# A second gather stage with ten slots, whose gather DMA adds onto loaded edge features

## The reference

```python
    def _L1_gnn_ref(x, edge_index, edge_attr, W, b, eps):
        src = edge_index[0]
        dst = edge_index[1]
        msg = jax.nn.relu(x[src] + edge_attr)
        agg = jax.ops.segment_sum(msg, dst, num_segments=x.shape[0])
        h = (1.0 + eps) * x + agg
        out = h @ W.T + b
        return jax.nn.relu(out)
...
    x = _layernorm(x + _L0_gnn_ref(x, edge_attr_64, ..., edge_index, batch0), axis=-1)
    x = _layernorm(x + _L1_gnn_ref(x, edge_index, edge_attr_64, L1_gnn_W, L1_gnn_b, L1_gnn_eps), axis=-1)
```

## Time and profile before

| | |
|---|---|
| time, median of 3 runs | 10885.92 us (10885.71 to 10889.72) |
| span of the profiled execution | 10892.7 us |
| second gather stage, first to last gather DMA | 6110.0 to 10760.8 us |
| GpSimd busy | 6799.3 us, 62% of the span |
| TensorE busy | 4140.9 us, 38% |
| VectorE busy | 2557.8 us, 23% |
| ScalarE busy | 1173.7 us, 11% |
| DMA engines, mean rate | 59 GB/s |

### The profile page before, as it was taken

How to read it: one execution, slowest core, us unless ns; L and a number is a source line. 1 busy time by engine, 2 the same in 40 slices (tenths; PEclk the granted TensorE clock), 3 DMA queues, 4 the chain that set the end, 5 groups by cost and what they waited for, 6 DMA issues and landing times. The chain is left out here.

```text
span 10892.7 us, 119855 instructions
## 1 busy us (share of the span) xinstructions
PE 4140.9 (38%) x36713; PEld 3322.5 (31%) x36713; DVE 2557.8 (23%) x7060; ACT 1173.7 (11%) x2055; POOL 6799.3 (62%) x6897
## 2 busy tenths in 40 slices
PE   4445444444444445445887311111111111111113
PEld 3333333333333333334776211111111111111112
DVE  2111111111111111114997311111111111111112
ACT  0000000000000000001334300000000000000001
POOL 5555555555555555556998466666666666666663
PEclk7655555656665655555555555555555555555555
DMA  2222222222222222222443111111111111111111
GB/s 78 60 61 61 61 61 60 61 61 61 61 61 61 61 60 61 61 61 75 125 123 114 50 44 44 43 45 44 44 44 44 44 43 45 44 43 45 44 44 35
DMA packets 882270, 637.83 MB, mean 59 GB/s; under 512 B 534579, under 2 KB 780831, under 8 KB 881496
## 3 DMA queue, kind: packets, MB, share of 16 engines
q1 hardware_dynamic: 590300, 326.49, 10.9%
q0 software_dynamic: 200416, 208.55, 10.2%
q10 hardware_dynamic: 91536, 102.58, 2.7%
HBM read 528.19 MB, written 108.90 MB: 58 GB/s over the span
## 5 line engine op out<-in xcount | busy, mean ns | idle before, releaser
L349 POOL DMA_INDIRECT Z<-in_x_dram,idx_ring x3125 | 2958.8, 947 | 2088.3 <-DVE idx_ring L526 1205.2
L1156 POOL DMA_INDIRECT X<-x_scratch,idx_ring x3125 | 2986.5, 956 | 1738.3 <-issue 893.5
L1185 PE MATMUL PS<-hot_c,msg_c 128*64 128x48 f32 x6250 | 811.6, 310 | 3865.8 <-ACT msg_c L1171 2630.0
L1185 PEld LDWEIGHTS PS<-hot_c,msg_c 128*64 128x64 f32 x6250 | 713.5, 223 | 3964.0 <-issue 2528.7
L401 PE MATMUL PS<-ZT,W_sb 128*64 128x256 f32 x2500 | 689.5, 647 | 2375.0 <-ACT ZT L451 2238.9
L515 DVE BATCH_NORM_STATS2 stats<-PS 128x320 f32 (+1 forms) x625 | 311.6, 499 | 3158.2 <-remote 2670.5
L1216 DVE TENSOR_TENSOR table<-table,PS 64x48 f32 x625 | 130.0, 208 | 3773.0 <-remote 1822.2
L401 PEld LDWEIGHTS PS<-ZT,W_sb 128*64 128x64 f32 x2500 | 183.7, 199 | 2637.2 <-ACT ZT L451 2488.9
L451 ACT ACTIVATE ZT<-PS 128x640 f32<-128x640 f32 x625 | 439.4, 703 | 4602.4 <-remote 4300.2
L391 PE MATMUL PS<-ident,Z 128*128 128x128 f32 x3125 | 845.7, 413 | 161.7 <-issue 158.6
L420 PE MATMUL PS<-W_sb,ZT 128*64 128x64 f32 x12500 | 877.7, 318 | 0.0
(11 more groups left out here) (140 smaller groups left out, 2682.9 us busy)
## 6 DMA issues: line engine op xcount, KB each, us to landing
Z<-in_edge_attr_dram SPq DMA_DIRECT2D x625, 160.0 KB
h_scratch<-h_ring ACTq DMA_DIRECT2D x625, 160.0 KB
h_turns<-h_scratch SPq DMA_DIRECT2D x125, 800.0 KB
E<-in_edge_attr_dram SPq DMA_DIRECT2D x625, 160.0 KB
Z<-in_x_dram,idx_ring POOLq DMA_INDIRECT x3125
X<-x_scratch,idx_ring POOLq DMA_INDIRECT x3125
x_nodes<-in_x_dram SPq DMA_DIRECT2D x1, 3125.0 KB
x_ring<-in_x_dram SPq DMA_DIRECT2D x25, 125.0 KB
```

Of the source, the lines that this page charges most:

```text
L349: nc.gpsimd.indirect_dma_start(out=Z[:, s, j, 0:D], out_offset=None, in_=x, in_offset=bass.IndirectOffsetOnAxis(ap=idx_ring[:, s, j:j + 1] ...
L1156: nc.gpsimd.indirect_dma_start(out=X[:, s, j, :], out_offset=None, in_=x1_dram, in_offset=bass.IndirectOffsetOnAxis(ap=idx_ring[:, s, j:j ...
L1185: last = nc.tensor.matmul(PS[D:P, s % 2, 0:WIN], msg[:, s, j, :], hot[:, s, j, :], start=(j == 0), stop=(j == TG - 1))
```

## The change

Only the second gather stage changes. The buffers E, msg and hot and the semaphores for loads and gathers have ten slots (RING) in place of five; X is gone. SyncE loads edge features up to ten groups ahead. GpSimd waits only until the edge features of its group have been loaded, and its indirect DMA, now with `compute_op=ALU.add`, adds the rows of x1 onto them in E. Its indices are read from `src_idx` where they lie, so its 3125 DMAs are written out one by one, without a loop, and `idx_ring` isn't used. ACT waits for the gather itself. DVE's add (L1208) and its index copy (L1211) are gone; DVE adds PE's result of a group onto the table five groups later, behind the one-hot matrix of the group now at hand. PE uses five PSUM banks. The other engines' loops cover two turns each (`loop_halves`).

```diff
-        gathered_x1 = [ctx.enter_context(nc.semaphore(f"gathered_x1{s}")) for s in range(S)]
+        gathered_x1 = [ctx.enter_context(nc.semaphore(f"gathered_x1{s}")) for s in range(2 * S)]
...
-            E = sb(here, "E", [P, S, TG, D])
-            X = sb(here, "X", [P, S, TG, D])
-            msg = sb(here, "msg_c", [P, S, TG, D])
-            hot = sb(here, "hot_c", [P, S, TG, WIN])
+            RING = 2 * S
+            E = sb(here, "E", [P, RING, TG, D])
+            msg = sb(here, "msg_c", [P, RING, TG, D])
+            hot = sb(here, "hot_c", [P, RING, TG, WIN])
...
                 @block.sync
-                        for s in range(S):
-                            reuse(sp, msg_ready[s], i)
-                            sp.dma_start(E[:, s, :, :], edge_v[i * S + s]).then_inc(e_loaded[s], 16)
+                        for s in range(S):
+                            r = half * S + s
+                            if later(i):
+                                sp.wait_ge(msg_ready, i * S + (s + 1 - RING))
+                            sp.dma_start(E[:, r, :, :], edge_v[i * S + s]).then_inc(e_loaded[r], 16)
...
                 @block.gpsimd
-                            reuse(pool, idx_ready[s], i)
-                            reuse(pool, sum_ready[s], i)
-                            carry_wait(pool)
-                            for j in range(TG):
-                                nc.gpsimd.indirect_dma_start(
-                                    out=X[:, s, j, :], out_offset=None, in_=x1_dram,
-                                    in_offset=bass.IndirectOffsetOnAxis(ap=idx_ring[:, s, j:j + 1], axis=0)
-                                ).then_inc(gathered[s], 16)
+                    for g in range(G):
+                        r = g % RING
+                        pool.wait_ge(e_loaded[r], 16 * (g // RING) + 16)
+                        carry_wait(pool)
+                        for j in range(TG):
+                            n = g * TG + j
+                            nc.gpsimd.indirect_dma_start(
+                                out=E[:, r, j, :], out_offset=None, in_=x1_dram,
+                                in_offset=bass.IndirectOffsetOnAxis(ap=src_idx[:, n:n + 1], axis=0),
+                                compute_op=ALU.add
+                            ).then_inc(gathered[r], 16)
...
                 @block.scalar
-                            act.wait_ge(sum_ready[s], i + 1)
-                            reuse(act, summed[s], i)
-                            act.activation(msg[:, s, :, :], E[:, s, :, :], ACT.Relu).then_inc(msg_ready[s], 1)
+                            act.wait_ge(gathered[r], n * (16 * TG) + 16 * TG)
+                            if later(i):
+                                act.wait_ge(summed, i * S + (s + 1 - RING))
+                            act.activation(msg[:, r, :, :], E[:, r, :, :], ACT.Relu).then_inc(msg_ready, 1)
...
                 @block.tensor
-                            reuse(pe, added, i * S + max(s - 1, 0))
+                            if not isinstance(i, int) or i >= 1:
+                                pe.wait_ge(added, i * S + (s + 1 - S))
                             for j in range(TG):
-                                last = nc.tensor.matmul(PS[D:P, s % 2, 0:WIN], msg[:, s, j, :], hot[:, s, j, :],
+                                last = nc.tensor.matmul(PS[D:P, s, 0:WIN], msg[:, r, j, :], hot[:, r, j, :],
                                                         start=(j == 0), stop=(j == TG - 1))
...
                 @block.vector
-                            dve.wait_ge(e_loaded[s], i * 16 + 16)
-                            dve.wait_ge(gathered[s], i * (16 * TG) + 16 * TG)
-                            nc.vector.tensor_tensor(E[:, s, :, :], X[:, s, :, :], E[:, s, :, :],
-                                                    ALU.add).then_inc(sum_ready[s], 1)
-
-                            nc.vector.tensor_copy(idx_ring[:, s, :],
-                                                  src_idx[:, ds(i * (S * TG) + (S + s) * TG, TG)]
-                                                  ).then_inc(idx_ready[s], 1)
+                    def turn(i, half, n):
                         firsts = windows_of_turn(dve)
                         for s in range(S):
+                            if s == S - 1:
+                                load_windows(dve, i)
+                            one_hot(i, half, s)
+                            add(i - 1, s, firsts[s])
```

More of the change, by code:

```diff
@@ L1184, in turn @@
                             for j in range(TG):
-                                last = nc.tensor.matmul(PS[D:P, s % 2, 0:WIN], msg[:, s, j, :], hot[:, s, j, :],
+                                last = nc.tensor.matmul(PS[D:P, s, 0:WIN], msg[:, r, j, :], hot[:, r, j, :],
                                                         start=(j == 0), stop=(j == TG - 1))
-                            last.then_inc(summed[s], 1)
-                    turn(0)
-                    with pe.Fori(1, SB) as i:
-                        turn(i)
+                            last.then_inc(summed, 1)
@@ L1193, in _, with one_hot @@
+                    turn(0, 0, 0)
+                    turn(1, 1, 0)
+                    loop_halves(pe, 2, SB, turn)
                 @block.vector
                 def _(dve):
-                    nc.vector.tensor_copy(idx_flat, src_idx[:, 0:S * TG]).then_inc(idx_first, 1)
-                    def turn(i):
-                        load_windows(dve, i)
+                    def one_hot(i, half, s):
+                        if later(i):
+                            dve.wait_ge(summed, i * S + (s + 1 - RING))
+                        nc.vector.tensor_tensor(
+                            hot[:, half * S + s, :, :], window[:, :].unsqueeze(1).to_broadcast([P, TG, WIN]),
+                            rel5[:, ds(i * S + s, 1), :].rearrange("p a t -> p (a t)").unsqueeze(2)
+                            .to_broadcast([P, TG, WIN]), ALU.is_equal).then_inc(hot_ready, 1)
@@ L1198, in turn, with add @@
+                    def add(i, s, first):
+                        dve.wait_ge(summed, i * S + s + 1)
+                        if not isinstance(i, int) or i * S + s > 0:
+                            dve.wait_ge(added, i * S + s)
+                        nc.vector.tensor_tensor(table[D:P, ds(first, WIN)], table[D:P, ds(first, WIN)],
+                                                PS[D:P, s, 0:WIN], ALU.add).then_inc(added, 1)
+                    def turn(i, half, n):
                         firsts = windows_of_turn(dve)
@@ L1214, in turn @@
-                            dve.wait_ge(summed[s], i + 1)
-                            reuse(dve, added, g)
-                            nc.vector.tensor_tensor(table[D:P, ds(firsts[s], WIN)], table[D:P, ds(firsts[s], WIN)],
-                                                    PS[D:P, s % 2, 0:WIN], ALU.add).then_inc(added, 1)
-                    turn(0)
-                    with dve.Fori(1, SB) as i:
-                        turn(i)
+                            if s == S - 1:
+                                load_windows(dve, i)
@@ L1224, in gnn_kernel @@
+                            one_hot(i, half, s)
+                            add(i - 1, s, firsts[s])
+                    load_windows(dve, 0)
+                    for s in range(S):
+                        one_hot(0, 0, s)
+                    turn(1, 1, 0)
+                    loop_halves(dve, 2, SB, turn)
+                    for s, first in enumerate(windows_of_turn(dve)):
+                        add(SB - 1, s, first)
         with ExitStack() as here:
```

47 lines of the change are left out of this document (18 added, 29 removed).

## The result

The changed kernel takes 12,054.75 us (median of 3 runs, 12,053.52 to 12,060.92) against 10,885.92 us: a ratio of 1.107 (95% interval 1.105 to 1.109), 1169 us slower. The prediction said 10,138 us, faster, in a range of 10,105 to 11,444 us. The profiled execution has a span of 12,051.7 us, 1159.0 us more than that of before.

A forecast was written before the change was run, and what follows sets the result against it. GpSimd, the busiest engine, was taken to stand still because DVE hands it indices late. Savings of 712 + 28 + 10 - 2 = 748 us off 10,885.9 gave 10,138 us, in a range of 10,105 to 11,444 us.

The forecast's parts named there:

- Term 4: GpSimd's adding gather DMAs: taken to cost no more than plain ones, 0 us, with 653 or 1306 us as dearer cases.
- dearer descriptors, a loss: Rival: each adding DMA costs GpSimd over 0.239 us more; at 0.418 us more the kernel takes 11,444 us; chance 0.20.
- the middle case: In Term 4: GpSimd writes three descriptors for two, 0.21 us more for each adding DMA, 653 us over 3125.
- Terms 1 and 2: Changed stage: GpSimd no longer waits for DVE, 712 us saved; five groups of slack cover PE's late results, costing nothing.
- GpSimd still pauses for PE: Rival: PE's results come only when GpSimd pauses, so more slots lengthen bursts; 10,494 or 10,850 us; chance 0.11.
- Term 3: DVE's add and index copy go, off the path; GpSimd's DMAs get 9 ns shorter, 28 us saved.
- Term 5: The adding itself on the DMA engines: hidden behind GpSimd's 1.25 us step even at three times 0.178 us, costing nothing.
- Term 6: Fetching GpSimd's 3125 written-out DMAs as code: taken to cost nothing, at most 36 us.
- Term 7: Stage start: GpSimd must wait until the first edge-feature load lands, 2 us lost, at most 3.
- Term 8: Stage end: 9.6 us from GpSimd's last DMA to the next stage in place of 19.33, 10 us saved.
- the DMA engines as the bound: Rival: adding a row costs the DMA engines 8.4 times a copied row or more, no gain or slower; chance 0.06.
- no effect: Rival: the change leaves the kernel's time as it was; chance 0.02.

The follow-up runs named there:

- e12: Changed kernel with six kinds of groups in turn: direct DMAs plain or adding, gathers of 128 or 16 rows plain or adding; 8996.4 us beside 9060 before.
- e15: Kernel before with the gather DMA adding onto loaded edge features, X and DVE's add gone; five slots, loop, index copies kept; 12,203.8 us, ratio 1.092.
- e13: Changed kernel with plain gathers into X and DVE adding them to E; ten slots, no index copies; 10,857.6 us beside 11,177 before, ratio 0.972.
- e1: Changed kernel without the DMA's add, edge features left out of the output; 9056.5 us beside 9045 before, ratio 1.001.
- e11: Changed kernel without the DMA's add, same kernel as e1 run again; 9069.2 us beside 9060 before, ratio 1.001.
- e5: Kernel before, unedited, run again and profiled; 11,171.7 us beside 11,156, ratio 1.001.
- e2: Changed kernel with plain gathers into X and DVE adding, same kernel as e13; 9036.5 us beside 9045 before, ratio 0.999.
- e14: Kernel before with GpSimd's DMAs written out, reading src_idx without index copies; five slots, DVE's add kept; 10,964.7 us beside 11,177, ratio 0.981.
- e16: Kernel before with only GpSimd's loop written out; index copies, five slots and DVE's add kept; 11,106.6 us beside 11,177, ratio 0.994.
- e6: Changed kernel, unedited, run again and profiled; 12,135.3 us beside 11,156 before, ratio 1.089.
- e7: Changed kernel with a group's five gathers differing in rows, width and whether they add; 11,345.4 us beside 11,156 before.
- e8: Changed kernel with four of a group's five gathers made direct DMAs, 128 or 64 rows, plain or adding; 9410.9 us beside 11,156 before.
- e9: Changed kernel with plain gathers into X and DVE adding, same kernel as e13; 9051.8 us beside 9060 before, ratio 0.999.

## Why the prediction was wrong

**Term 4, the adding DMA, is the step that failed.** It was taken as 0 with an upper bound of 0.418 us, and measured 1.557 - 0.944 = 0.613 us. Put in at (1.558 - 0.947) x 3125 = 1909 us, the sum gives 10,138 + 1909 = 12,047 us, against 12,055. Two thoughts in it were wrong. "Writing descriptors seems cheap against the fixed part" is true (1.0 ns a row), but I took from it that the add would be cheap; the add makes the fixed part itself longer, by 0.45 us. And the upper bound was the difference between a gather and a direct DMA, which holds only what gathering costs. The add costs GpSimd something that gathering does not contain; direct DMAs pay it as well (e12), and no row of before bounded it. What GpSimd does in that time stays open. The rival "dearer descriptors, a loss" had the mechanism, the decisive point (0.239 us) and a chance of 0.20, but a time that was 611 us short.

The rule set against term 4, the Trainium skill's Collectives: The Full Stack, "The bandwidth ceiling: the fold count and why AG ≠ RS ≠ AR" (two read descriptors for a reduced chunk, half the rate), agrees in size for the DMA engines here, though that page speaks of the reduce step of collectives. The gathers' queue takes 0.144 x 12,051.7 = 1735 us of each engine; less the first stage's half of the earlier trace rows, 555 us, that is 1180 / 3125 = 0.378 us for an adding gather against 0.178, 2.1 times. The packets of a gather also went from 16 to 128 at the same bytes, and the trace doesn't tell which of the two makes it. For GpSimd's own time, the middle case that I drew from it (0.21 us) was a third of what was measured.

**Terms 1 and 2 came true for another reason.** The wait for DVE did vanish in the changed kernel (issue 950.9 us, nothing behind DVE). But e15 shows that it vanishes with five slots too once a DMA adds, and e13 that with ten slots and plain gathers 584 us of waiting are left, and 319 us are gained. So had the add been free, the forecast of 10,138 us (748 us less) would probably still have missed in condition B; that is argued from e13, which keeps DVE's add, since the changed kernel without the add ran only in A (e1, e11). "A latency of up to 21.4 us" that 31 us of cover outlasts does not describe e13: there PE's instructions go out slowly through the whole burst, at 0.7 to 1.4 us each 14 to 28 us for the 20 of a group, an estimate, against GpSimd's 6.25 us, and no number of slots covers a rate (table adds waited up to 27.0 us). In the kernel before itself only the late result is seen, and the run doesn't say whether it is a latency. The pauses left in e13, one in eight groups (78 in 625), are my rival "GpSimd still pauses for PE"; it priced what is left at 356 of 712 us, and e13 had 584 left, where the kernel before in B had 902 beyond the issue gaps (e5). It had 0.11 and should have had far more, with the row in hand in which the wait ended only after GpSimd's last DMA.

**Term 3** (28 us for DVE's add being away) is not borne out: the plain gather takes 961 ns in the mean without DVE's add (e1) and 956 with it (e2). **Term 5** was right: the DMA engines have room, with 0.378 us of each engine for a gather in a step of 1.863 us. **Term 6** was right: no gap beyond 0.305 us, for 32 more instruction packets on q14 and one on q8. The prediction read q8 alone, whose packets are of 16 KB (0.13 MB in 8); the new code came over q14, whose packets are of 8 KB (0.08 MB in 10 before, 0.34 MB in 42 now). **Term 7**: 2.1 us, forecast 2. **Term 8**: 7.99 us to the next stage, forecast 9.6. The rivals of the DMA engines as the bound and of no effect did not come.

## What to carry to other kernels

Count what a change does to the engine that sets the pace before counting what it frees elsewhere: here a quarter microsecond more on each of 3125 DMAs was the break-even, and moving an add of 484 ns a group off an idle DVE cost GpSimd five times 613 ns. When no row prices an operation, a bound taken from a neighbouring operation is no bound; the wide range should go beyond it, or the chance to the losing side should be higher. And ask of a late result whether it is a latency (more buffers cover it) or a rate (they only put it off): in e13 the spacing of PE's instructions within a group told that it was a rate there.

Of the kernels tried none beats the one before in both conditions; ten slots with DVE's add (e13) is 2.8% faster in B and the same in A.

## What was not expected of the hardware

- An adding DMA costs GpSimd about 0.45 us more once and 1.1 ns for each row (e12; in the stream of 128-row gathers 0.944 to 1.557 us), and its queue carries 128 packets a gather where the plain one has 16: 200,416 to 550,416, (550,416 - 200,416) / 3125 = 112 more each.
- Direct DMAs of GpSimd overlap and leave work behind: a plain one of 64 rows took 1604 ns behind an adding one, so durations of mixed kinds mislead.
- The same kernel took 9045 or 11,170 us by the session, one chip showing both, with all DMAs equally long. In B, with GpSimd streaming plain gathers, table adds start up to 20 us after matmuls that were recorded back to back (before, e5, e14, e16), or PE's loads and matmuls themselves go out 0.7 or 1.4 us apart (e13, the only one); with adding gathers, or a mix (e6, e7, e8, e15), neither was seen. B's traces also hold about a quarter of A's semaphore updates where all gathers are plain (36,990 in e13, 143,885 in e9). What sets the condition, and what holds PE back, no run here has shown.
